# Attention halves on one core: order of values and maxima, and the output normalised by GpSimd with inverses repeated by a DMA

## The reference, cut to what matters

```python
xn = group_norm(x2, gn_scale, gn_bias)
q, k, v = heads(w_qkv @ xn + b_qkv)          # 8 heads of 32 channels
weight = softmax(einsum('bct,bcs->bts', q * scale, k * scale))
a = einsum('bts,bcs->bct', weight, v)
out = x2 + w_proj @ a + b_proj
```

## Time and profile before

| | us |
|---|---|
| three runs | 1919.38, 1919.95, 1920.85; median 1919.95 |
| the profiled execution | 1922.28 |
| its span in the profile | 1920.5, mean granted clock of PE 0.941 |
| L0, L1 and the first window's preparation | to about 364 |
| L2, the 16 windows | about 364 to 1486 |
| L3 | the rest |

### The profile page before, as it was taken

How to read it: one execution, slowest core, us unless ns; L and a number is a source line. 1 busy time by engine, 2 the same in 40 slices (tenths; PEclk the granted TensorE clock), 3 DMA queues, 4 the chain that set the end, 5 groups by cost and what they waited for, 6 DMA issues and landing times.

```text
span 1920.5 us, 37066 instructions
## 1 busy us (share of the span) xinstructions
PE 1666.5 (87%) x15160; PEld 768.6 (40%) x15160; DVE 1376.5 (72%) x2121; ACT 790.9 (41%) x1546; POOL 1360.7 (71%) x581
## 2 busy tenths in 40 slices
PE   6898656799999999999999999999997689889974
PEld 2333223344344444444444444444442355555541
DVE  5767577887777777777777777777771157878875
ACT  0443410255445455454454455454555233333320
POOL 0584500298888878878878878788689068988996
PEclk8898877799999999999999999999998889999986
DMA  5000030300001001010010010010010201222211
GB/s 189 1 2 1 1 129 0 146 15 24 2 23 45 2 24 45 2 46 23 1 60 9 2 67 2 1 67 2 2 46 1 89 29 52 84 82 75 74 51 47
DMA packets 48431, 75.10 MB, mean 39 GB/s; under 512 B 30804, under 2 KB 31110, under 8 KB 48262
## 3 DMA queue, kind: packets, MB, share of 16 engines
q1 hardware_dynamic: 38758, 72.15, 10.5%
q10 hardware_dynamic: 9504, 0.59, 0.3%
HBM read 44.87 MB, written 25.17 MB: 36 GB/s over the span
## 4 chain that ended last, share of the span: by engine, by line
PE 57%; DVE 30%; issue 5%; ACT 3%; POOL 2%; DMA 2%; SPq 0%; POOLq 0%; DVEq 0%; ACTq 0%
DVE MX L1327 18%; PE AV L684 8%; PE RB L932 6%; PE AV L945 3%; PE S L632 3%; PE S L720 3%; PE RB L720 3%; PE RB L981 3%; DVE HI L1304 2%; DVE LO L1305 2%; PE RB L710 2%; PE RB L738 2%; PE RB L745 1%; PE S L606 1%; PE S L960 1%
## 5 line engine op out<-in xcount | busy, mean ns | idle before, releaser
L1238 POOL TENSOR_TENSOR ACC<-ACC,PR 128x1024 f32<-128x1024 f32 x360 | 843.7, 2386 | 25.6 <-ACT PR L1075 25.3
L1075 ACT ACTIVATE PR<-S 128x512 f32<-128x512 f32 x687 | 388.7, 603 | 383.8 <-PE S L670 258.2
L1327 DVE TENSOR_REDUCE MX<-S 128x1 f32<-128x512 f32 x660 | 431.5, 681 | 103.7 <-PE S L632 56.0
L1238 POOL TENSOR_TENSOR ACC<-PR 128x1024 f32<-128x1024 f32 x72 | 169.6, 2379 | 351.7 <-PE S L699 156.3
L684 PE MATMUL AV<-PR,VT 128*32 128x512 f32 x2304 | 306.1, 609 | 2.3 <-ACT PR L1075 2.3
L632 PE MATMUL S<-HI 32*128 32x512 f32 x660 | 259.6, 483 | 17.5 <-DVE MX L1327 11.3
L1075 ACT ACTIVATE PR<-RB 128x512 f32<-128x512 f32 x316 | 187.8, 603 | 101.8 <-PE S L670 42.0
L1327 DVE TENSOR_REDUCE MX<-RB 128x1 f32<-128x512 f32 x300 | 201.3, 680 | 22.3 <-PE RB L632 13.9
L655 PE MATMUL S<-HI 32*128 32x512 f32 x687 | 194.7, 467 | 2.8 <-DVE X L1520 2.3
L632 PEld LDWEIGHTS S<-HI 32*128 32x128 f32 x660 | 106.1, 188 | 189.5 <-DVE MX L1327 84.4
L1264 POOL TENSOR_TENSOR PR<-WO,WRK 128x1792 f32<-128x1792 f32 x32 | 155.4, 4877 | 29.6 <-DMA WO<-WO 17.4
(11 more groups left out here) (352 smaller groups left out, 3477.4 us busy)
## 6 DMA issues: line engine op xcount, KB each, us to landing
X<-out_y SPq DMA_DIRECT2D x24, 1024.0 KB, 4.9
out_y<-X SPq DMA_DIRECT2D x16, 1024.0 KB, 4.7
X<-in_x SPq DMA_DIRECT2D x8, 1024.0 KB, 8.5
OHU<-out_y SPq DMA_DIRECT2D x8, 512.0 KB, 4.0
X<-out_y SPq DMA_DIRECT2D x8, 512.0 KB, 4.0
out_y<-X SPq DMA_DIRECT2D x8, 512.0 KB, 3.1
out_y<-OHU SPq DMA_DIRECT2D x8, 512.0 KB, 3.2
WO<-WO SPq DMA_DIRECT2D x128, 16.0 KB, 1.8
```

What stands on the lines that cost most here:

```text
L1075: nc.scalar.activation(exps(s, pair)[:, HALF * one:HALF * one + HALF], RING[ring.place()], ACT.Exp, scale=1.0 if i is None else float(D) * ...
L1238: nc.gpsimd.tensor_tensor(ACC[:, pair, :], so_far, exps(s, pair), ALU.add).then_inc(pool_used, 1)
L1327: nc.vector.tensor_reduce(out=MX[:, h, t, keys:keys + 1], in_=bank(), op=ALU.max, axis=AX.X).then_inc(ring_free, 1)
```

## The change

`window_jobs` now orders the jobs of a step itself, with the values as a job ("values", n): in step 0 of a half the two waves of maxima come first, ahead of the other jobs; steps 1 to 6 keep first wave, jobs, values, second wave; in step 7 it is first wave, values of step 6, second wave, negate, the other jobs, values of step 7, flip. In the L2 windows the job "settle" takes the place of "spread": it takes no bank, PE and DVE do nothing in it, ACT issues at step 5 a DMA that repeats each head's row of inverses on its 32 partitions (RC to the new INV), and POOL multiplies OH by INV behind its additions of step 6 and raises norm_done. The L0 windows keep "spread". The statistics of ahead=2 move from steps 11 and 13 to 9 and 12.

```diff
@@ -35,6 +35,7 @@
 SUM_AT = 1
 INVERT_AT = 3
 RETURN_AT = 4
+REPEAT_AT = 5
 SPREAD_AT = 6
 NHEAD = C // D
 EPS = 1e-5
@@ -110,8 +111,8 @@
 
     if job[0] == "v":
         return 2 if single else 1
-    return {"max": 2, "late": 2, "stats": 0, "negate": 0, "reread": 0, "concepts": 4, "softmax": 0, "turn": 4,
-            "classes": 2, "norms": 2, "pool": 0, "regate": 0, "write": 4}.get(job[0], 1)
+    return {"max": 2, "late": 2, "stats": 0, "negate": 0, "values": 0, "reread": 0, "concepts": 4, "softmax": 0, "turn": 4,
+            "settle": 0, "classes": 2, "norms": 2, "pool": 0, "regate": 0, "write": 4}.get(job[0], 1)
 
 
 def wait(eng, sem, value):
@@ -129,25 +130,17 @@
     return [("max", half, n) for n in range(4 * TILES_HALF)]
 
 
-def window_jobs(post=False, nxt=True, gn=False, ahead=0, trail=True, single=False, side=()):
+def window_jobs(post=False, nxt=True, gn=False, ahead=0, trail=True, single=False, side=(), settle=False):
 
 
 
 
     jobs = [[] for _ in range(STEPS)]
-    late = [[] for _ in range(STEPS)]
     for half in range(2):
         first = MT * half
-        if half == 0 or nxt:
-            waves = maxima(1 - half)
-            for step in range(first, first + MT):
-                jobs[step].append(waves.pop(0))
-                late[step] = [("late",) + waves.pop(0)[1:]]
-            jobs[step] += late[step] + [("negate", 1 - half)]
-            late[step] = [("flip", 1 - half)]
         if half == 1 or trail:
             jobs[first + SUM_AT].append(("sums",))
-            jobs[first + SPREAD_AT].append(("spread", half - 1))
+            jobs[first + SPREAD_AT].append(("settle" if settle else "spread", half - 1))
     if nxt:
         for step, job in zip((1, 2, 3, MT + 3) if single else (2, 4, MT + 2, MT + (3 if gn else 4)), QK_ORDER):
             jobs[step].append(("qk",) + job)
@@ -157,15 +150,28 @@
         for step, job in zip((3, 5, MT + 4, MT + 7), ((0, 0), (1, 0), (0, 1), (1, 1))):
             jobs[step].append(("post",) + job)
     if ahead:
-        first = MT + 3 if ahead == 2 else MT
+        first = MT + 1 if ahead == 2 else MT
         jobs[first].append(("stats", 0, ahead))
-        jobs[first + (2 if ahead == 2 else 1)].append(("stats", 1, ahead))
+        jobs[first + (3 if ahead == 2 else 1)].append(("stats", 1, ahead))
         jobs[first + (4 if ahead == 2 else 3)].append(("gn", 0, ahead))
     if gn:
         jobs[MT + 5].append(("gn", 1, 1))
     for step, stage in side:
         jobs[step].append(stage)
-    return [job + waves for job, waves in zip(jobs, late)]
+    for half in range(2):
+        waves = maxima(1 - half) if half == 0 or nxt else []
+        for at in range(MT):
+            first, second, rest = waves[:1], [("late",) + wave[1:] for wave in waves[1:2]], jobs[MT * half + at]
+            waves = waves[2:]
+            ends = [("negate", 1 - half)] if first else [], [("flip", 1 - half)] if first else []
+            if at == 0:
+                rest = first + second + rest
+            elif at < MT - 1:
+                rest = first + rest + [("values", 0)] + second
+            else:
+                rest = first + [("values", 0)] + second + ends[0] + rest + [("values", 1)] + ends[1]
+            jobs[MT * half + at] = rest
+    return jobs
 
 
 
@@ -434,9 +442,10 @@
             u = 2 * i + 2
             last = isinstance(i, int) and i == B - 1
             first = isinstance(i, int) and i == 0
-            window(u, 0, window_jobs(post=not first, gn=True, ahead=int(first), trail=not first), i)
-
-            window(u + 1, 1, window_jobs(nxt=not last, ahead=0 if last else 2), i)
+            window(u, 0, window_jobs(post=not first, gn=True, ahead=int(first), trail=not first,
+                                      settle=True), i)
+
+            window(u + 1, 1, window_jobs(nxt=not last, ahead=0 if last else 2, settle=True), i)
 
         TILES = MT * B
         P_DMAS = PAIRS
@@ -748,22 +757,16 @@
                 for s in range(STEPS):
                     ring.begin(jobs[s], i is None)
                     scores(u, par, s)
-                    last = s % MT == MT - 1
-                    behind = [job for job in jobs[s] if job[0] == ("flip" if last else "late")]
-                    for job in jobs[s][:len(jobs[s]) - len(behind)] + [("values",)] + behind:
+                    for job in jobs[s]:
                         if job[0] == "values":
-
-                            if s % MT:
-                                values(u, par, s - 1)
-                            if last:
-                                values(u, par, s)
+                            values(u, par, s - 1 + job[1])
                         elif job[0] == "spread":
                             spread(2 * u + job[1])
                         elif job[0] == "sums":
                             sums(2 * u - 1 + s // MT)
                         elif job[0] == "max" or job[0] == "late":
                             max_scores(u + 1 - job[1], par if job[1] else 1 - par, *job[1:])
-                        elif job[0] == "negate" or job[0] == "stats":
+                        elif job[0] in ("negate", "stats", "settle"):
                             pass
                         elif job[0] == "flip":
                             flip(u + 1 - job[1], job[1])
@@ -1051,6 +1054,12 @@
                 act.dma_start(RC[0:P:D, :].rearrange("h (p c) -> h p c", p=D),
                               R16[:, :]).then_inc(inverse_in, 16)
 
+            def repeat_inverse(n):
+
+                wait(act, inverse_in, 16 * (n + 1))
+                act.dma_start(INV[:, :],
+                              RC[0:P:D, :].unsqueeze(1).broadcast_to([H, D, HALF])).then_inc(repeat_in, 16)
+
             def window(u, par, jobs, i):
                 early = par == 1 and i is None
                 for s in range(STEPS):
@@ -1085,6 +1094,9 @@
                         return_inverse(2 * u - 1)
                     if s == MT + RETURN_AT:
                         return_inverse(2 * u)
+                    for half in range(2):
+                        if s == MT * half + REPEAT_AT and ("settle", half - 1) in jobs[MT * half + SPREAD_AT]:
+                            repeat_inverse(2 * u + half - 1)
                     if early:
                         for stage in jobs[s]:
                             after(0, stage)
@@ -1237,6 +1249,12 @@
                                 so_far = ACC[:, pair, :]
                             nc.gpsimd.tensor_tensor(ACC[:, pair, :], so_far, exps(s, pair),
                                                     ALU.add).then_inc(pool_used, 1)
+                    if jobs and ("settle", half - 1) in jobs[s]:
+
+                        own, n = par if half else 1 - par, 2 * u + half - 1
+                        wait(pool, repeat_in, 16 * (n - 3))
+                        nc.gpsimd.tensor_tensor(OH[own][1 - half], OH[own][1 - half], INV[:, :],
+                                                ALU.mult).then_inc(norm_done, 1)
                     if jobs and ("gn", 1, 1) in jobs[s]:
                         if i < B - 1:
                             norm_apply(i + 1)
@@ -1402,8 +1420,12 @@
                     for job in jobs[s]:
                         if job[0] == "spread":
                             normalise(1 - par if job[1] else par, 1 if job[1] else 0)
+                        elif job[0] == "settle":
+                            pass
                         elif job[0] == "sums":
                             ring.skip(1)
+                        elif job[0] == "values":
+                            pass
                         elif job[0] == "max" or job[0] == "late":
                             row_max(*job[1:])
                         elif job[0] == "negate":
```

More of the change, by code:

```diff
@@ L239, in program @@
         RC = sb("RC", [P, HALF])
+        INV = sb("INV", [P, HALF])
         R16 = sb("R16", [P, HALF // D])
@@ L390, in program @@
         inverse_in = sem("inverse_in")
+        repeat_in = sem("repeat_in")
         norm_done = sem("norm_done")
```

## The result

The changed kernel takes 2023.4 us (four runs, 2018.7 to 2026.8) against 1920.4 us for the kernel before in the same runs: ratio 1.0533, 95% interval 1.0511 to 1.0555. It is slower by about 103 us; the forecast was 2032 us, 1985 to 2066.

The account below looks back on a forecast made before the run. PE (87% busy) and POOL (71%) both counted before; afterwards a loop of POOL and ACT was to bound each half. 1922.3 + 69 (wait) + 44 (clock) = 2035, 2033 by the median, said as 2032 us; range 1985 to 2066.

Parts of the forecast that it names:

- (e): Product by INV on POOL behind step 6's additions: 1.29 us; ACT's next copy of AV waits for it, +69 us.
- A1: Second half of a batch's four, in the window of parity 0; forecast to take 39.0 us.
- B0: Third half of a batch's four, first of parity 1; forecast 37.15 us, in the last batch about 33.4.
- B1: Fourth half of a batch's four, second of parity 1; forecast to take 37.15 us.
- A0: First half of a batch's four, in the window of parity 0; forecast to take 37.15 us.
- (b): Normalisation off DVE and statistics moved: 2 us gained in each of 7 B1 halves, on PE's side only.
- The ring's length: Loop POOL, ACT's copy and first exponential, PE, sums, POOL, once a half: 150.45 us a batch against 141.1.
- from there to POOL's next start: 6.7 us: From PE going on after ACT's first exponential, through v product and sums, to POOL's next half: 6.7 us.
- (f): PE's granted clock falls after long waits: 2 us lost in each of 22, +44 us, bounds 0 and 75.
- (c): Values between last step's maxima, maxima ahead of step 0's v product: taken as 0, at best 0.5 us a half gained.
- (a): Spread gone from PE: 1.2 us a half, at most 38 us over 31 halves if PE stays the bound.
- (d): Copy of the inverses to 128 partitions: about 0.55 us of ACT's queue; taken as 0, up to 1 us a half.

## Why the prediction was right

**The wait (e).** Right in place, sign and waiter. The product was put at 1.29 us and took 1.28. The copy of AV was put at 29.3 us behind POOL's start, 33.3 in A1: it comes at 29.3 and 33.25, and at 30.9 in the A1 of the last batch, which has no normalised input. PE's waits were forecast less well. In front of A1, B0 and B1 they are 1.2, 5.6 and 3.3 us where I had 1.7, 5.4 and 4.0. In front of A0, at the end of B1, the wait is 2.0 us where I had 4.9: "4 us and more in three halves of four" holds for one half of four. PE comes to the end of B1 some 3 us later than I put it, and that is (b) for the most part, below. By itself it doesn't change the half's length, because POOL and ACT set it.

**The ring's length** was a little too long. The term "from there to POOL's next start: 6.7 us" was read from a step 1 with the old order, of 5.00 us; with both late maxima ahead of the v product, DVE has them done in time, and step 1 takes 4.07. A half at full clock is 36.3, not 37.15, and A1 38.6, not 39.0, so a batch is 147.5 and not 150.45: +6.4 us, where I had 9.35.

**The clock (f)** was a little too small: 154.6 less 147.5 is 7.1 us a batch, where I had three waits at 2 us each, so 6. By halves the loss is 1.0 (A0), 1.9, 2.6 and 1.6 us. Where A0 ends PE waits just 1.24 us, and in five of seven batches the clock falls there too, in two not. The two errors cancel in part, 13.5 us a batch against 15.35, which is luck; so the five like batches came 9 us below the forecast. The last batch made up 3 of them: its B0 was put at 33.4 us with no loss of clock behind it, but PE waits 9.6 us there, the granted clock from 1556 to 1562 is 0.50, and B0 takes 36.2.

**The statistics (b)** were wrong in sign, and hidden by the wait. With the wait relaxed, B1 takes 34.7 to 36.3 us with them in steps 9 and 12 and 33.95 in the old steps 11 and 13; the 2 us gained in each B1 aren't there in any run with the places of the change. The step that failed is "the second still beside a q/k product. I take 2 us gained": in step 12 DVE has four maxima (0.6 us each, 2.4), the split (1.5) and the statistics (1.5), more than the 4.8 us of the step, and the two light steps behind can't make it up. I also passed over that the small step "gn" moves with them from 15 to 13. **The order (c)**, taken as 0, is about 0 in steps 0 and 1 together and 0.3 us to the bad in most last steps; in the one pair of runs that compares it without the spread, with statistics in steps 8 and 9, it is to the good. **The spread (a)**: step 6 takes 2.70 us after, 1.29 less, and once the wait is gone it shows: 141.1 to 136.7 us a batch with the statistics in their old places, which is four times 1.29 less what the last steps cost. **The DMA (d)** costs ACT nothing that shows. Its copy is there about 7 us behind the issue: with the product earlier, POOL begins it 7.0 us behind the issue in the closest cases and has waited for the DMA 13 times, 3.1 us in all. In the changed kernel POOL comes 11.2 us behind the issue or later and never waits; DVE in step 6 did.

## What to carry to other kernels

When an operation moves to another engine, ask first what stands before it on the new queue and who waits for its signal: here 1.3 us behind 28 us of additions became a loss of 103 us, and the same operation two additions earlier, or with a wait looser by one count, none. A wait that is stricter than the data needs can cost nothing until its signal becomes late; look for such waits when a signal changes hands. And where light and heavy steps alternate, put extra DVE work where the step's length exceeds DVE's own sum, and count the sum.

## What was not expected of the hardware

A DVE product of 128x512 with both inputs in SBUF took 0.69 us with POOL idle, 2.39 in the mean of 29 and 7.59 at most beside POOL's two-input additions, and was over 0.55 to 0.61 us behind the end of one of them; that was 3 to 6% of the kernel for one operand in 36 instructions. How long PE waits did not by itself tell whether its clock falls: behind 1.24 us it fell in five of seven batches, behind about 0.7 us of it, after 4.6 us of filler, in four batches and not in two. Work without use on a waiting PE made the kernel 27 and 42 us faster. A repeat of four rows to 128 partitions, 256 KB by DMA within SBUF, ran at 49 GB/s with a DMA share of 0.24, about four of 16 engines; another pattern of the same copy was not tried.
